# The mixer of a four-layer block makes y by channels, with two heads side by side in TensorE, and VectorE masks the attention maxima

## The chip, the cores and the metric

The kernel runs on one core of a Trainium2 chip. The metric is the device time of one execution in microseconds (us), from its first to its last instruction and the little that lies around them. The kernel before took 2301.28 us (median of 3 runs, 2294.27 to 2305.86).

## The reference

1024 tokens (two sequences of 512) of width 512 go through four layers, each as x = layernorm(x + layer(x)): causal attention with 32 heads of 16, a linear layer with summed binary weights, a state-space mixer, and a linear layer with two chosen low-rank experts. The change touches the attention and, mostly, the mixer. The mixer, per sequence, with H = 128 heads of P = 64 channels, state N = 128, and 8 groups that share B and C (the kernel works in chunks of 128 tokens where the reference has 32; the sum is the same):

```
dt  = softplus(dt + dt_bias);  cum = cumsum(dt * A) inside a chunk
scores[i,j,h] = (C_i . B_j) * exp(cum_i - cum_j) * dt_j      for j <= i
y[i,h,:]      = sum_j scores[i,j,h] * x[j,h,:]               # inside the chunk
              + exp(cum_i,h) * (C_i . state_h)               # carried from earlier chunks
              + D_h * x[i,h,:]
state_h      <- exp(cum_last) * state_h + sum_j dt_j exp(cum_last - cum_j) x_j B_j
g = y * silu(gate);  g = g * rsqrt(mean over the group of g^2 + eps) * norm_w
out = g @ out_w.T
```

x, B and C come out of a projection, a causal convolution with four taps and a SiLU. The gate is another projection of the same input.

## The kernel before

Every engine runs its own program, written out by hand, and they meet only at semaphores. After the attention (16 passes, one for each sequence and key head, to about 306 us) and the linear layer (to about 418 us) comes the mixer, lines 1079 to 1613, to about 2214 us, and then the experts.

The mixer has 8 groups of 16 steps; six of the groups are a loop in the program. A group is two halves of 8 heads (512 channels); a half has 8 chunks of 128 tokens, c = 0 to 7, and c = 0 and c = 4 begin a sequence, so that 12 of 16 steps carry a state in and 12 feed one. I call the steps of a group k = 0 to 15. In a step TensorE does, in this order: for the first half the chunk's B transposed and the product C.B (`cb`, L1269, L1270); the gate of these tokens (`p_gate`, 12 products of fp32r parts, L92); the transposes of the step before's y (`flip_y`, L1240); the carried part C times state for 8 heads at once (`p_inter`, L1284); the projection of one tile of channels for the next half (`p_mix` from `w_x`; in four of 16 steps one of B or C as well); the out-projection of the step before (`p_out`); the new state (`p_state`, L1300); the transposes of the next step's x (`flip_x`, L1231); and the scores times x, one product per head, tokens by 64 channels (`p_intra`, L1310).

Tokens lie on the partitions in y, so the sum with D x (`xskip`) and the product with the gate follow directly (L1539, L1543), and y must be turned into channels (`flip_y`) before it is split into high and low part (`yT`, L1347 and L1441) and projected out. The decays of a step are `cum_all`, 512 KB that a DMA spreads over the partitions, held against the step's own cum by VectorE (`arguments`, L1431), through Exp on ScalarE (8 instructions, L1368), times cb on GpSimd (L1596). ScalarE needs its Exp table for these and its Silu table for the gate and for x (L1375, L741), so it loads a table twice in every step. The first step of each half also splits the half's out-weights (`out_low_part` on VectorE, L1412), the last one the next half's gate weights (`gate_low_part` on GpSimd, L1563).

In the attention (lines 98 to 570) the row maxima are taken from scores that TensorE masks by adding a product of an identity and a mask (L276); VectorE reduces a bank that holds one or two heads (`read_fill`, L445). The scores that become probabilities are made apart, the other way round, and masked likewise (L288). The maxima of the next pass are made while this pass runs: `columns` (L455, L457) ends them, and `flip_max` (L266) needs them.

## Time and profile before

| | |
|---|---|
| median of 3 runs | 2301.28 us |
| the profiled execution | 2301.09 us, its span 2299.3 us |
| TensorE busy | 2129.1 us, 93% |
| VectorE busy | 1659.0 us, 72% |
| ScalarE busy | 1442.3 us, 63% |
| GpSimd busy | 1128.9 us, 49% |
| mean granted TensorE clock | 0.964 |

The profiled execution is one of the same kernel on the chip; its span runs from the first to the last instruction. PE is TensorE (PEld its weight loads), DVE VectorE, ACT ScalarE, POOL GpSimd, SP SyncE, which issues the DMAs. A row of a timeline gives start and length; an x16 merges sixteen instructions, and the time in square brackets is how long the engine had been idle before them and what ended it. A 32-bit product appears as two matmul records, so that the eight heads of L1310 are x16. Two records in a row overlap at their ends, so the cost of work is read from start to next start.

### The profile page before, as it was taken

What the parts mean: (1) busy time and instruction counts of PE and PEld (TensorE: products, weight loads), DVE (VectorE), ACT (ScalarE), POOL (GpSimd) and SP (SyncE); (2) the same over time, 40 slices, a digit from 0 to 9 for tenths busy, and PEclk for the clock granted to TensorE, in tenths of its full rate; (3) what the DMA queues carried; (4) which work ended last, traced back from release to release, by engine and by line L of the source; (5) the groups of instructions that cost most, each with busy time, mean ns of one, the idle gap of its engine ahead of it and who ended that gap; (6) DMA issues with size and microseconds to landing.
All of it is one profiled execution on the core that took longest, in us unless ns stands there. A gap on an engine that the chain in (4) does not pass through costs nothing. (4 is left out here: it accounts for less than half of the span.)

```text
span 2299.3 us, 35192 instructions
## 1 busy us (share of the span) xinstructions
PE 2129.1 (93%) x11224; PEld 1665.0 (72%) x11224; DVE 1659.0 (72%) x2544; ACT 1442.3 (63%) x2823; POOL 1128.9 (49%) x974
## 2 busy tenths in 40 slices
PE   8999997799999999999999999999999999999868
PEld 4666665677778777777787777777777777777645
DVE  4666565678877787778777876787787778777766
ACT  1455523567667766767677667667766776677631
POOL 3444230355555654555555645554656465545531
PEclk9899987899999999999999999999999999999979
DMA  4000010312121212121212122112221222121110
GB/s 156 1 0 0 0 51 19 94 61 92 47 87 56 83 47 88 65 83 41 93 57 83 46 87 83 70 45 89 70 69 62 73 70 72 58 71 59 46 36 37
DMA packets 72235, 140.72 MB, mean 61 GB/s; under 512 B 34449, under 2 KB 35473, under 8 KB 67826
## 3 DMA queue, kind: packets, MB, share of 16 engines
q1 hardware_dynamic: 72050, 138.44, 18.2%
q8 instruction: 93, 1.52, 0.3%
q14 instruction: 92, 0.75, 0.1%
HBM read 134.74 MB, written 3.67 MB: 60 GB/s over the span
## 5 line engine op out<-in xcount | busy, mean ns | idle before, releaser
L92 PE MATMUL p_out<-w_out,yT 128*128 128x512 f32 x1536 | 387.9, 403 | 44.8 <-DVE yT L1441 38.6
L92 PEld LDWEIGHTS p_out<-w_out,yT 128*128 128x128 f32 x1536 | 296.4, 194 | 120.0 <-DVE yT L1441 43.3
L92 PE MATMUL p_mix<-x_high,w_x 128*128 128x512 f32 x1024 | 381.5, 434 | 1.4 <-DVE x_low L1017 1.4
L1596 POOL TENSOR_TENSOR wq_t<-wq_t,cb 128x1024 f32<-128x1024 f32 x128 | 325.0, 2539 | 107.9 <-DVE cb L1486 95.7
L753 DVE SCALAR_TENSOR_TENSOR conv<-p_mix,unit_small,conv 128x511 f32<-128x511 f32 (+2 forms) x384 | 287.2, 748 | 95.0 <-ACT conv L733 85.9
L92 PE MATMUL p_gate<-w_gate,x_high 128*128 128x512 f32 x1024 | 341.4, 415 | 14.8 <-POOL w_gate L1563 14.8
L1368 ACT ACTIVATE wq_t<-wq_t,minus_cum 128x128 f32<-128x128 f32 x1024 | 313.9, 389 | 1.4
L741 ACT ACTIVATE x_channels<-conv 128x512 f32<-128x512 f32 x128 | 80.7, 630 | 266.6 <-DVE conv L753 265.9
L1310 PEld LDWEIGHTS p_intra<-x_dt,wq_t 128*128 128x128 f32 x2048 | 241.2, 192 | 2.4
L1310 PE MATMUL p_intra<-x_dt,wq_t 128*128 128x64 f32 x2048 | 242.7, 272 | 0.0
L1441 DVE TENSOR_TENSOR yT<-p_flip,yT 128x512 fp32r<-128x512 f32 x128 | 88.4, 691 | 213.6 <-ACT yT L1347 213.6
L92 PEld LDWEIGHTS p_mix<-x_high,w_x 128*128 128x128 f32 x1024 | 193.7, 189 | 61.9 <-issue 22.2
L92 PEld LDWEIGHTS p_gate<-w_gate,x_high 128*128 128x128 f32 x1024 | 190.5, 196 | 53.1 <-POOL w_gate L1563 17.0
L1584 POOL TENSOR_TENSOR x_to_state<-x_tokens,group_dt_end 128x512 f32<-128x512 f32 x96 | 102.8, 1071 | 245.3 <-ACT x_tokens L1339 233.9
L1431 DVE TENSOR_TENSOR wq_t<-cum_all,group_logs 128x1024 f32<-128x1024 f32 x128 | 219.4, 1714 | 2.6 <-DMA cum_all<-cum_rows 1.3
L772 POOL TENSOR_TENSOR w_x<-w_raw_tiles,w_x 128x512 fp32r<-128x512 f32 x64 | 87.4, 1366 | 251.1 <-DVE w_x L761 251.0
L92 PE MATMUL p_gate<-w_gate,x_low 128*128 128x512 f32 x512 | 207.4, 405 | 0.0
L92 PE MATMUL p_mix<-x_low,w_x 128*128 128x512 f32 x512 | 201.0, 393 | 0.0
L1588 POOL TENSOR_TENSOR x_dt<-x_tokens,group_dt 128x512 f32<-128x512 f32 x128 | 144.3, 1127 | 99.6 <-PE p_intra L1310 99.3
L1591 POOL TENSOR_TENSOR x_skip<-x_tokens,group_skip 128x512 f32<-128x512 f32 x128 | 182.9, 1429 | 1.0 <-DVE y L1539 1.0
L733 ACT ACTIVATE conv<-p_mix,unit_small 128x512 f32<-128x512 f32 x128 | 99.6, 778 | 114.2 <-PE p_mix L92 112.2
L1375 ACT ACT_TABLE_LOAD x128 | 164.2, 1283 | 5.8 <-DVE y L1543 3.7
(227 smaller groups left out, 4255.0 us busy)
## 6 DMA issues: line engine op xcount, KB each, us to landing
cum_all<-cum_rows SPq DMA_DIRECT2D x128, 512.0 KB, 3.7
w_staged<-in_w_gate SPq DMA_DIRECT2D x16, 1024.0 KB, 5.9
w_raw_tiles<-in_w_x SPq DMA_DIRECT2D x64, 256.0 KB, 3.4
w_staged<-in_w_out SPq DMA_DIRECT2D x16, 1024.0 KB, 4.9
w_raw_tiles<-in_w_bc SPq DMA_DIRECT2D x16, 256.0 KB, 2.8
x<-in_x SPq DMA_DIRECT2D x1, 2048.0 KB, 17.4
out<-z SPq DMA_DIRECT2D x8, 256.0 KB, 2.0
wqkv<-in_wqkv SPq DMA_DIRECT2D x4, 384.0 KB, 6.3
```

The lines of the kernel that those rows point to most:

```text
L92: last = pe.matmul(dst, left[a](k), right[b](k), start=k == 0 and n_ == 0, stop=stop and k == tiles - 1 and n_ == 2)
L733: act.activation(self.conv[:, par], self.p_mix[:, bank], ACT.Identity, bias=w[:, TAPS:TAPS + 1], scale=w[:, TAPS - 1:TAPS]).then_inc(self. ...
L753: m = dve.scalar_tensor_tensor(self.conv[:, par, back:], self.p_mix[:, bank, 0:SEQ - back], w[:, TAPS - 1 - back:TAPS - back], self.conv[: ...
L1310: m = pe.matmul(p_intra[:, h * HEAD_P:(h + 1) * HEAD_P], decay[:, k % 2, h], xdt[:, h], start=True, stop=True)
L1368: m = act.activation(decay[:, k % 2, h], decay[:, k % 2, h], ACT.Exp, bias=neg[:, c, head:head + 1])
L1375: act.activation(sg[:], p_gate[:], ACT.Silu).then_inc(sg_done, 1)
L1431: dve.tensor_tensor(decay[:, k % 2], cumB[:], over(logs[:, 0, c, mine], P), ALU.min).then_inc(arg_done, 1)
L1441: dve.tensor_tensor(yT[:, 1].rearrange("p j t -> p (j t)"), p_flip[:], yT[:, 0].rearrange("p j t -> p (j t)").bitcast(F32), ALU.subtract). ...
L1584: pool.tensor_tensor(xs[:], xtok[:], over(dtend[:, c, mine], HEAD_P), ALU.mult).then_inc(xs_done, 1)
L1588: pool.tensor_tensor(xdt[:], xtok[:], over(dtg[:, c, mine], HEAD_P), ALU.mult).then_inc(xdt_done, 1)
L1591: pool.tensor_tensor(xskip[:], xtok[:], over(dg[:, mine], HEAD_P), ALU.mult).then_inc(xskip_done, 1)
L1596: pool.tensor_tensor(decay[:, k % 2], decay[:, k % 2], cb[:, c].unsqueeze(1).to_broadcast([P, UNIT_HEADS, P]), ALU.mult).then_inc(decay_do ...
```

## The change

In the mixer y is made with channels on the partitions. Each head's product is turned round: x (times dt) is the stationary operand, 64 columns wide, and the head's 128 x 128 scores stream through. Even heads write partitions 0 to 63 of the new bank `p_y`, odd heads 64 to 127. The carried state goes the same way into the same bank, as eight products of state (64 columns) with `Ce`, which is C times exp(cum): exp(cum) is written to DRAM once, at the end of the linear layer, fetched with 512 KB per step, and multiplied by C on GpSimd. So `p_inter`, two VectorE passes over it and the addition are gone, and `flip_y` with them. In exchange the gate is flipped: after SiLU, TensorE transposes it back into its own bank `p_gate`, from where VectorE multiplies it into y; `p_gate` is therefore free only when y is done. The sum of squares, before one ScalarE instruction with an accumulator, is now Square on ScalarE, a reduction over four tiles on VectorE, and a product with a column of ones on TensorE (`sum_squares`). y is one buffer where it was two.

The order of a step changes too. The projection of x channels comes first in it, cb has its own bank, ScalarE does the decays of an even step in the odd step before, after its `last_tap`, and those of an odd step at the end of the even step before, so that a table is loaded once per step; `out_sum` moves behind y. One B/C projection moves from step 0 to step 2.

In the attention the mask products of the maxima go. VectorE adds the mask from a table (`row_mask`) and takes the maximum in one instruction per head, which writes its sum back to PSUM.

```diff
-                        last = pe.matmul(pF[:, b, (i + 1) * wide - P:(i + 1) * wide], ident_b[:], mask_b[:],
-                                         start=False, stop=True)
...
+                        for n_, r in enumerate(heads):
+                            m = dve.tensor_tensor_reduce(pF[:, b, n_ * wide:(n_ + 1) * wide],
+                                                         pF[:, b, n_ * wide:(n_ + 1) * wide],
+                                                         row_mask[:, CPS * P - wide:], 1.0, MASKED, ALU.add, ALU.max,
+                                                         top[:, qc, r:r + 1])
+                        m.then_inc(f_dve, 1)
...
+                sp.wait_ge(soft, 6)
+                for u in range(2 * GROUPS):
+                    sp.dma_start(keep["exp_cum_dram"][u].rearrange("c h t -> h c t"),
...
+                act.activation(dabs[:], cum[:], ACT.Exp, scale=-1.0).then_inc(soft, 1)
...
-                        wait(pe, sg_done, s)
+                        wait(pe, y_done, s)
                         split_product(pe, p_gate[:], ...
...
-                            pe.matmul(p_inter[:], BC[:, 1, cols], state[:].rearrange("p h e -> p (h e)"),
-                                      start=True, stop=True).then_inc(inter_done, 1)
+                            for h in range(UNIT_HEADS):
+                                m = pe.matmul(p_y[sides(h), h // 2], state[:, h], Ce[:, h], start=h < 2, stop=False)
+                            m.then_inc(inter_done, 1)
...
+                        pe.wait_ge(sg_done, s + 1)
+                        for j in range(UT):
+                            m = pe.transpose(p_gate[:, j * P:(j + 1) * P], sg[:, j * P:(j + 1) * P], ident[:])
...
+                            sum_squares(*before)
...
-                            m = pe.matmul(p_intra[:, h * HEAD_P:(h + 1) * HEAD_P], decay[:, k % 2, h], xdt[:, h],
-                                          start=True, stop=True)
+                            m = pe.matmul(p_y[sides(h), h // 2], xdt[:, h], decay[:, k % 2, h],
+                                          start=not carries(c) and h < 2, stop=h >= UNIT_HEADS - 2)
...
+                        if k % 2 and k + 1 < STEPS:
+                            exponentials(s + 1, k + 1)
...
+                        dve.tensor_tensor(y[:], p_y[:], xd[:], ALU.add).then_inc(y_sum, 1)
+                        dve.wait_ge(sg_flipped, s + 1)
+                        dve.tensor_tensor(y[:], y[:], p_gate[:].rearrange("p (j t) -> p j t", j=UT), ALU.mult).then_inc(y_done, 1)
+                        if started and before[1] >= CHUNKS:
+                            out_sum(*before)
...
+                            pool.wait_ge(in_exp_cum, (n_carries(g, k) + 1) * 16)
+                            pool.tensor_tensor(Ce[:], Ce[:], BC[:, 1, cols].unsqueeze(1).to_broadcast([P, UNIT_HEADS, P]),
+                                               ALU.mult).then_inc(ce_done, 1)
```

TensorE, one step of the first half, from one scores product to the next. Before:

```order
L1310 MATMUL p_intra<-x_dt,wq_t 128x64 x8
L1269 MATMUL p_mix<-ident,bc_channels 128x128
L1270 MATMUL p_mix<-bc_channels 128x128
L92 MATMUL p_gate<-w_gate,x_high 128x512 x2
...
L1240 MATMUL p_flip<-ident,y 128x128 x4
L1284 MATMUL p_inter<-state,bc_channels 128x512
L92 MATMUL p_mix<-x_high,w_x 128x512
...
L92 MATMUL p_out<-w_out,yT 128x512 x12
L1300 MATMUL p_state<-x_to_state,b_tokens 128x512
L1231 MATMUL p_flip<-ident,x_channels 128x128 x4
```

And now, in the same step (`wq_t` is the buffer of the decays, `square_sums` the squares summed over four tiles):

```order
L1334 MATMUL p_y<-wq_t,x_dt 64x128 x8
L92 MATMUL p_mix<-x_high,w_x 128x512
...
L1286 MATMUL p_small<-ident,bc_channels 128x128
L1287 MATMUL p_small<-bc_channels 128x128
L92 MATMUL p_gate<-w_gate,x_high 128x512 x2
...
L1301 MATMUL p_y<-c_decayed,state 64x128 x8
L92 MATMUL p_out<-w_out,y_parts 128x512 x12
L1311 MATMUL p_gate<-ident,silu_gate 128x128 x4
L1319 MATMUL p_state<-x_to_state,b_tokens 128x512
L1263 MATMUL p_small<-one_column,square_sums 128x1
L1244 MATMUL p_flip<-ident,x_channels 128x128 x4
```

The x projection went from the middle of the step to its start, the out-projection stands where it stood in time, and behind it now come the gate's transposes, which wait for ScalarE.

ScalarE, an odd step (between two Silu of gates). Before:

```order
L1368 ACT_TABLE_LOAD
L1368 ACTIVATE wq_t<-wq_t,minus_cum 128x128 x8
L1375 ACT_TABLE_LOAD
L1375 ACTIVATE silu_gate<-p_gate 128x512
L1344 REGISTER_ALU
L1347 ACTIVATE yT<-p_flip 128x512
L1349 ACTIVATE y,sum_squares<-y 128x512
```

And now, from the end of an even step through the odd one:

```order
L1371 ACT_TABLE_LOAD
L1371 ACTIVATE wq_t<-wq_t,group_logs 128x128 x8
L1385 ACTIVATE y_parts<-y 128x512
L722 REGISTER_ALU
L724 ACTIVATE conv<-p_mix,unit_small 128x512
L1368 REGISTER_ALU
L1371 ACTIVATE wq_t<-wq_t,group_logs 128x128 x8
L1389 ACTIVATE y<-y 128x512
L1435 ACT_TABLE_LOAD
L1435 ACTIVATE silu_gate<-p_gate 128x512
```

Two steps' decays now stand in a row ahead of the odd step's Silu, and one table load of each kind serves two steps.

VectorE, where a half's first step ends (k = 8) and the next begins:

```order
L1585 TENSOR_TENSOR y<-p_y,x_skip 128x512
L1588 TENSOR_TENSOR y<-y,p_gate 128x512
L1466 SCALAR_TENSOR_TENSOR w_out<-w_staged,unit_small,w_out 128x512 x4
L1485 TENSOR_TENSOR wq_t<-cum_all,group_logs 128x1024
L1494 TENSOR_TENSOR y_parts<-y,y_parts 128x512
```

This order is as before (L1539, L1543, L1412, L1431, L1441); what changed is that the arguments in its fourth row now feed decays that ScalarE makes ahead of its Silu.

## Rows read from the trace of the kernel before

**Rows 1.** The mixer: window, length, busy us of PE, PEld, DVE, ACT, POOL (records), clock, DMA.
```profile
424.00:2214.00 1790.00, 1698.23 (x8544) 1360.86 (x8545) 1356.27 (x1892) 1237.88 (x2414) 963.66 (x679) 0.98 0.21 68
```

**Rows 2.** TensorE's waits in the mixer: us in total, times, longest us.
```profile
PE p_out L92 <- DVE yT L1441: 38.6, 18, 3.5
PE p_flip L1240 <- ACT x_tokens L1339: 18.4, 24, 1.2
PE p_gate L92 <- POOL w_gate L1563: 14.8, 7, 5.0
```

**Rows 3.** Timeline, TensorE, an ordinary step: start us, us, line, shapes, count.
```profile
1216.14 1.02 PE L1300 MATMUL p_state<-x_to_state,b_tokens 128*128 128x512 f32 x2
1216.99 0.60 PE L1231 MATMUL p_flip<-ident,x_channels 128*128 128x128 f32 x4
1217.43 1.90 PE L1310 MATMUL p_intra<-x_dt,wq_t 128*128 128x64 f32 x16
1219.14 0.71 PE L92 MATMUL p_gate<-w_gate,x_high 128*128 128x512 f32 x2
...
1221.99 0.60 PE L1240 MATMUL p_flip<-ident,y 128*128 128x128 f32 x4
1222.42 1.02 PE L1284 MATMUL p_inter<-state,bc_channels 128*128 128x512 f32 x2
```

**Rows 4.** Timeline, TensorE, 32-column products of attention, and what follows.
```profile
149.87 2.36 PE L299 MATMUL pO<-probsT,v_ones 128*32 128x512 f32 x32
152.17 0.63 PE L266 MATMUL pF<-ident,max_cols 128*68 128x128 f32 x4
```

**Rows 5.** Timeline, TensorE, the start of a group of 16 steps.
```profile
1095.55 0.65 PE L1231 MATMUL p_flip<-ident,x_channels 128*128 128x128 f32 x4 [1.52 <-ACT x_channels L741]
...
1098.61 1.22 PE L92 MATMUL p_gate<-w_gate,x_high 128*128 128x512 f32 x2 [2.08 <-POOL w_gate L1563]
...
1103.76 0.60 PE L1240 MATMUL p_flip<-ident,y 128*128 128x128 f32 x4
```

**Rows 6.** Timeline, VectorE, the first step of a half ends, k = 8.
```profile
1221.24 6.45 DVE L1412 SCALAR_TENSOR_TENSOR w_out<-w_staged,unit_small,w_out 128x512 fp32r<-128x512 f32 x4
1227.61 1.21 DVE L1431 TENSOR_TENSOR wq_t<-cum_all,group_logs 128x1024 f32<-128x1024 f32 x1
```

**Rows 7.** Timeline, ScalarE, the same place.
```profile
1222.12 2.46 ACT L1368 ACTIVATE wq_t<-wq_t,minus_cum 128x128 f32<-128x128 f32 x8
1224.59 1.28 ACT L1375 ACT_TABLE_LOAD   x1
1225.89 0.60 ACT L1375 ACTIVATE silu_gate<-p_gate 128x512 f32<-128x512 f32 x1
1226.38 0.59 ACT L1347 ACTIVATE yT<-p_flip 128x512 fp32r<-128x512 f32 x1
```

**Rows 8.** Timeline, VectorE, row maxima of one pass of attention.
```profile
151.09 0.18 DVE L457 SCALAR_TENSOR_TENSOR max_cols<-row_max,max_cols 128x16 fp32r<-128x16 f32 x1
...
156.80 2.15 DVE L445 TENSOR_REDUCE row_max<-pF 128x2 f32<-128x256 f32 x4 [0.57 <-PE pF L276]
...
163.71 1.29 DVE L445 TENSOR_REDUCE row_max<-pF 128x1 f32<-128x512 f32 x2 [0.41 <-PE pF L276]
165.03 0.18 DVE L455 TENSOR_SCALAR max_cols<-row_max 128x16 fp32r<-128x16 f32 x1
```

**Rows 9.** Groups by line and shape: busy us, mean ns, idle before, releaser.
```profile
L1596 POOL TENSOR_TENSOR wq_t<-wq_t,cb 128x1024 f32<-128x1024 f32 x128 | 325.0, 2539 | 107.9 <-DVE cb L1486 95.7 <-ACT wq_t L1368 11.5
...
L1349 ACT ACTIVATION_READ_ACCUMULATOR y<-y 128x1 f32 x128 | 25.9, 202 | 0.0
```

**Rows 10.** Timeline, SyncE's queue, ScalarE and TensorE, before and at the mixer's start.
```profile
394.08 5.66 SPq L859 DMA_DIRECT2D cum_rows<-cum  x16
...
417.17 0.63 ACT L741 ACTIVATE bc_channels<-conv 128x512 f32<-128x512 f32 x1 [1.86 <-DVE conv L753]
...
424.78 1.23 PE L92 MATMUL p_gate<-w_gate,x_high 128*128 128x512 f32 x2 [4.95 <-POOL w_gate L1563]
```


## What I predict, and why

> **What bounds the kernel now.** I read the busy times by stretch first, then TensorE's waits, then the timelines of single steps. The mixer takes 1790 us of 2299.3, and TensorE is busy for 1698 of them [rows 1], so it bounds this stage and waits only some 92 us. The reader should see that 95% of the stage can be changed only by changing TensorE's own work, and that the other engines (1356, 1238 and 964 us) matter where they come late. The list of waits says where that is: 38.6 us for the low part of y, 18.4 for ScalarE to free the transposes' bank, 14.8 for the gate weights of a new half [rows 2]. At the start of a group the timeline has 1.52 and 2.08 us of idle time, and then the gate's 12 products take 5.15 us, from 1098.61 to 1103.76, with the clock fallen to the lower of its two levels [rows 5]. In the ordinary step the gate's products take 2.85 us, 1219.14 to 1221.99 [rows 3]. I call a stage's sum a ledger per group; there are eight groups.
>
> **TensorE's own work in a step.** Prices go from start to next start [rows 3]. The scores times x: 1217.43 to 1219.14, 1.71 us for 16 records, 0.107 each. The carried part has the shape of the state product, two records of 512 columns: 0.85 us (1216.14 to 1216.99). Four transposes: 0.44 us (1216.99 to 1217.43), 0.11 each. The flips of y go and the flips of the gate come, 0.44 against 0.44.
>
> Turned round, a head has 128 columns to stream and not 64, in two records. A 512-column record costs 0.425, so 128 columns cost 0.107, and eight heads one after the other would cost 16 x 0.107 = 1.71 us, the same as now. If two heads run side by side it is 0.85. The trace has such products in the attention: 32 records, four heads in 32 columns each, 512, 384, 256 and 128 columns long, in 2.36 us [rows 4]. One after the other these 1280 columns for four heads in two records would be 8 x 1280/512 x 0.425 = 8.5 us; side by side 2.13. So they run side by side, and I take 0.85 us for two halves of the array. The next product of full width starts 2.30 us after the first narrow one, 0.17 above 2.13. That is the price of leaving the narrow form, some of which (0.11) is the last record's own streaming beyond what I count; entering it is not shown by a row, since attention waits for ScalarE there. The nearest row for a drained engine is that a record of 1.90 us of work for 1.71 us of starts ends 0.19 after the next begins [rows 3]; so entry lies between 0 and 0.19, and I take 0.27 for a visit, with 0.12 and 0.36 as ends.
>
> What the Trainium skill says of this, in TensorEngine Tiling (Array Packing), Key Properties, is that changing the tiling mode drains the engine, not only a change of tile. By that rule the entry is paid in full. Its price here would be the 0.19 above, and the visits' sum 0.36 each; without it 0.12. The rows here show the way out alone, so the rule stands untested for the way in, and it speaks against this change, which makes 224 visits.
>
> So, over 128 steps, of which 96 carry: scores 128 x (1.71 - 0.85 - 0.27) = -75 us. Carried part 96 x (0.85 + 0.27 - 0.85) = +26. Sum of squares: one product with one column, two records that each load 128 columns of weights; the transposes' 0.11 each is the nearest row, 0.22 a step, +28. Together -21 us of TensorE work. With visits at 0.12 it is -55, at 0.36 -1.
>
> **Waits of TensorE in the mixer.** What goes, per group: the flips of y waited 18.4/8 = 2.3 for their bank [rows 2]; x has it alone now. At the group's start 1.52 + 2.08 of idle time and 2.3 of slow clock [rows 5] go as they are, since the x projection now stands ahead of the gate. The waits for y's low part (38.6/8 = 4.8) and some 1.9 of slow clock behind them (my estimate, less than the 2.3 of rows 5) end too, to be counted anew. Sum 14.9.
>
> What comes. I lay a step out from T, the end of a scores product. y is summed and multiplied in 1.6 us of VectorE (1024 columns cost 1.21 [rows 6], the rest is for semaphores), which the x projection covers (12 products like the gate's: 2.75 when nothing is waited for), so the new wait of the gate for `y_done` costs nothing in a plain step. In a half's first step VectorE then splits the out-weights for 6.45 us, and the arguments take 1.21 more [rows 6]; with GpSimd less busy the split is shorter at k = 0, so I put the arguments' end at T + 9.1. y's low part follows at 9.8, against an out-projection that is due at 2.75 + 0.25 for cb (two short products of 0.11 and a little) + 2.85 for the gate + 1.1 for the carried part = 6.9: a wait of 2.9. Behind it ScalarE, which took the decays of the step after next (2.46) only at 9.1, makes y's high part (0.59), loads a table (1.28) and makes the Silu (0.5 from start to next start) [rows 7], by T + 13.9, while the gate's flips are due at 6.9 + 2.9 + 2.75 = 12.6: 1.3 more. So 4.2 us at k = 1 and 4.2 at k = 9. At k = 15 the decays wait for the next group's tables behind `out_sum` and the logs, and Silu is 1.7 late. At k = 8 the gate weights are late by 2.2, since GpSimd now has C times exp(cum), 2.5 us as for the decays [rows 9], and D x ahead of them. At k = 0 I leave 2.7 of the 3.6 us that stood idle there [rows 5], as the loop's own branch and refetch, which no change of order covers, and 0.8 for cb: 3.5. In the other odd steps Silu is ready at T + 9.5 with 9.4 to 9.6 wanted: 0.9 in all. Slow clock after the two long waits: 1.0. Sum 17.7, or 2.8 more than what goes: +22 us. The mixer so comes out at +1.
>
> Not on the path: 96 more products on GpSimd, 96 x 2.54 = 244 us on top of 964 in 1790 [rows 1, 9]; the fetch of C's factor, which by the same layout has some 7 us for 512 KB; ScalarE's 1.28 of table load per step, which it gains as slack.
>
> **The mixer's ends.** Before it, exp(cum) needs a table load of 1.28 and about 1.1 us on ScalarE behind its last Silu, which started at 417.17, and then 16 DMA issues; the 16 of cum took 5.66 us of SyncE's queue [rows 10]. The mixer starts 8 us later. Its first gate waited until 424.78 for weights, 4.95 us idle, and 2.75 us of x projection now fill that. At the end the sum of squares and `out_sum` come one after another, an estimated 1.4. Together +7 (4 to 10).
>
> **The attention.** One pass's maxima on VectorE take from 156.80 to 165.03, 8.2 us, with waits for TensorE among them (0.57 and 0.41 in two rows) [rows 8]. The next pass's first transposes started at 152.17 though the maxima's columns were done at 151.27: TensorE was the later one by 0.9 us [rows 4, 8]. Without the masks TensorE is earlier, so VectorE's chain is late next. Sixteen single maxima: they read 4 x 1280 = 5120 columns. 512 columns cost 0.54 in the row of four (2.15/4) and 0.65 in that of two (1.29/2), so 5.4 to 6.5; I take 6.4, since half of the new ones are shorter than that. Each new instruction has a second one that reads the accumulator out. VectorE has no such row; ScalarE's takes 0.20 [rows 9] and its next starts about 0.1 later. Bounds are 0.05 and 0.35, and I take 0.15: 2.4 us, with 0.4 for counters. That is 9.2, 1.0 longer than now, less the 0.9 of slack, and a little for semaphores: +0.3 a pass, +5 us in 16. With 0.05 it is -15, with 0.35 +50 (3.2 x 16).
>
> For the same instruction the Trainium skill, Vector Engine (DVE) Microarchitecture Reference, section 5.2, gives 1.04 ns per column and about 75 ns per instruction. An estimate by that page is 5.3 + 32 x 0.075 = 7.7 us and the attention would gain about 13 us, the kernel end at 2294.
>
> **Sum.** 2301.1 (the profiled execution; the median of the runs is 2301.3) - 21 + 22 + 7 + 5 = 2314. I say 2312.
>
> **The rivals.** 1. *TensorE gains what it should.* A visit costs 0.12 and not 0.27, -34 us, and the new waits come to no more than the old ones, -22: 2314 - 56 = 2258. For it: 2.30 us against a floor of 2.13 is all that a row shows of the cost of a visit, and ScalarE, relieved of 128 x 1.28 us, is seldom late. Against it: the waits are worked out from places where ScalarE and VectorE are in series.
> 2. *VectorE becomes the bound of attention.* Reading out each maximum costs 0.35, and a pass takes 3 us longer: 2312 + 46 = 2358, slower. It decides from the point where sixteen maxima take over 9.1 us. For it: VectorE is in series with the flips now. Against it: small VectorE instructions in a row are short (L457 0.18).
> 3. *The flipped gate holds TensorE.* Each odd step waits 1 us for Silu behind two steps' decays: 7 more per group, +50: 2362. For it: the margin is 0.1 us. Against it: only if every instruction of ScalarE runs at its lone length.
> 4. *Two heads do not run side by side.* Then each of 224 visits costs 0.85 more, +190: 2502. The 2.36 us speak against it.
>
> **How the numbers follow.** The forecast of 2312 (2290 to 2335 by itself) has 0.36, rival 1 0.32, rival 2 0.16, rival 3 0.13, rival 4 0.03. 0.5% is 11.5 us, about what a measurement can tell from no change; so same is 2290 to 2313. Faster: 0.30 of rival 1, 0.05 of the forecast, 0.01 of others, 0.36. Same: 0.16 of the forecast and 0.04 of the rest, 0.20. Slower 0.44. The range of 2245 to 2368 leaves out the lower tail of rival 1, rival 4 and what of rivals 2 and 3 goes together.
>
> **What would show it.** From a step's first scores record to the next product: 1.1 us (0.95 if rival 1, 2.0 if rival 4). The sum-of-squares product costs 0.22. TensorE's waits in the mixer are near 110 us, most of them for y's low part and the Silu at k = 1 and 9. The mixer begins near 426. An attention pass takes 14.4 us and not 14.1; VectorE stands without a gap in its maxima. I am wrong if TensorE waits for C's factor, if the gate waits for y in plain steps, or if table loads are still two per step.

## The result, and the profile after

The changed kernel takes 2466.39 us (median of 4 runs, 2464.25 to 2470.53) against 2299.41 us before on the same chip: a ratio of 1.0736, 95% interval 1.0706 to 1.0766. I had forecast 2312 us with a range up to 2368. Slower was the likeliest direction by a little, but for a loss of this size I had only the case in which two heads do not run side by side, and that is not what happened.

| stage of the profiled execution | before | after | difference | forecast |
|---|---|---|---|---|
| to the first product behind the attention | 299.3 | 282.0 | -17.3 | +5 |
| from there to the first scores product | 136.5 | 138.2 | +1.7 | +7 with the end |
| mixer, first to last scores product | 1771.3 | 1953.9 | +182.6 | +1 |
| the rest, to the end of the span | 92.2 | 94.7 | +2.5 | |

The mixer on the changed kernel, window, length, busy us of PE, PEld, DVE, ACT, POOL (records), clock, DMA; it answers to [rows 1]:

```profile
413.00:2385.00 1972.00, 1743.69 (x10137) 1345.02 (x10137) 1611.12 (x1821) 1067.75 (x2156) 1240.42 (x774) 0.95 0.27 87
```

In this window, which is 182 us longer than that of [rows 1], VectorE is busy for 1611 us where it was 1356, and GpSimd for 1240 where it was 964. TensorE's busy time grew by only 45, and its mean granted clock fell from 0.98 to 0.95. TensorE's waits, us in total, times, longest us, answer to [rows 2]:

```profile
PE p_out L92 <- DVE y_parts L1494: 92.3, 43, 3.9
PE p_out L92 <- issue: 56.6, 15, 5.4
PE p_gate L92 <- POOL w_gate L1610: 25.6, 11, 2.7
PE p_mix L92 <- POOL w_x L763: 12.2, 16, 0.9
PE p_gate L1311 <- ACT silu_gate L1435: 11.8, 17, 1.3
```

The wait of the out-projection for y's low part is 92.3 us where it was 38.6. The row below it, with "issue", is the same wait at k = 9 and k = 1: the out-projection at 1285.18 starts 0.1 us after VectorE's low part ended at 1285.08, and has no other releaser. So 149 us, where it was 45 before. The flips of y are gone, as foreseen; the gate's flips wait 11.8 us in all. Two rows are waits for GpSimd itself, for weights that it splits: 37.8 us, where it was 14.8.

I add the mixer up over the 127 steps between the first and the last scores product: idle gaps of TensorE 221 us (before 87), everything else 1732 (before 1682). The 50 us of the second part are the granted clock. It stands at the lower of its two levels for 188 us of this stretch, where it did for 68 before, and TensorE is busy for 172 and 61 of them. The twelve records of the out-projection at k = 9 take 5.46 us at the lower level (it fell at 1284.5, while TensorE stood idle, and rose at 1291.3), and 2.91 in another step at the upper one. If I put the cost of the lower level at half of the busy time in it, which is an estimate, it is 86 us where it was 31: 55 more. The rest of the work is then some 5 us less than before.

**TensorE's own work.** The timeline around two scores products (start us, us):

```profile
1338.31 0.28 PE L1263 MATMUL p_small<-one_column,square_sums 128*128 128x1 f32 x2
1338.45 0.63 PE L1244 MATMUL p_flip<-ident,x_channels 128*128 128x128 f32 x4
1339.01 1.09 PE L1334 MATMUL p_y<-wq_t,x_dt 128*64 128x128 f32 x16
1340.04 0.50 PE L92 MATMUL p_mix<-x_high,w_x 128*128 128x512 f32 x1
1340.37 0.39 PE L92 MATMUL p_mix<-x_low,w_x 128*128 128x512 f32 x1
...
1345.46 0.39 PE L92 MATMUL p_gate<-w_gate,x_low 128*128 128x512 f32 x1
1345.78 1.09 PE L1301 MATMUL p_y<-c_decayed,state 128*64 128x128 f32 x16
1346.80 0.50 PE L92 MATMUL p_mix<-x_high,w_bc 128*128 128x512 f32 x1
1347.14 0.39 PE L92 MATMUL p_mix<-x_low,w_bc 128*128 128x512 f32 x1
```

The scores take 1.03 us to the next start (1340.04 - 1339.01), and the first wide record behind them starts its successor after 0.33 where a record in a row needs 0.23: 0.10 more. In front of them 0.20 us pass from the start of the last flip to the first scores record, in every step, where 0.11 passed before: 0.09 more. That is 1.22 in all. The carried product costs 1.02 and loses 0.09 in front of it (1345.46 to 1345.78, where 0.23 is usual) and 0.11 behind it: 1.22 as well. The forecast had 1.12 for each, 0.85 and 0.27 for the visit to narrow products; the 0.37 measured is the upper end that I gave (0.36). The sum of squares is 0.14 us, and the flip behind it takes 0.03 longer than its followers: 0.17, forecast 0.22. With these prices the three terms are 128 x (1.22 - 1.71) + 96 x (1.22 - 0.85) + 128 x 0.17 = -5 us, forecast -21. Two heads do run side by side, but a visit costs more than I took. The Trainium skill says in TensorEngine Tiling (Array Packing), Key Properties, that a change of mode drains the engine. The rows agree: the way in costs 0.09 us in front of both kinds of narrow product, and the way out 0.10 to 0.11.

**Where the time went.** A step of a second half, k = 10, VectorE:

```profile
1294.89 0.69 DVE L1588 TENSOR_TENSOR y<-y,p_gate 128x512 f32<-128x512 f32 x1
1295.50 0.75 DVE L1516 SCALAR_TENSOR_TENSOR acc<-p_out,inv_rms,acc 128x512 f32<-128x512 f32 x1
1296.28 2.55 DVE L1519 SCALAR_TENSOR_TENSOR acc<-attn,inv_rms,acc 128x512 f32<-128x512 f32 x1
1298.75 3.40 DVE L1485 TENSOR_TENSOR wq_t<-cum_all,group_logs 128x1024 f32<-128x1024 f32 x1
1302.07 1.52 DVE L1494 TENSOR_TENSOR y_parts<-y,y_parts 128x512 fp32r<-128x512 f32 x1
1303.52 0.74 DVE L744 SCALAR_TENSOR_TENSOR conv<-p_mix,unit_small,conv 128x511 f32<-128x511 f32 x1
```

and GpSimd in the same time:

```profile
1294.88 1.04 POOL L1636 TENSOR_TENSOR x_dt<-x_tokens,group_dt 128x512 f32<-128x512 f32 x1
1295.88 2.40 POOL L1640 TENSOR_TENSOR c_decayed<-c_decayed,bc_channels 128x1024 f32<-128x1024 f32 x1
1298.24 2.83 POOL L1645 TENSOR_TENSOR wq_t<-wq_t,cb 128x1024 f32<-128x1024 f32 x1
1301.03 2.02 POOL L1649 TENSOR_TENSOR x_skip<-x_channels,group_skip 128x512 f32<-128x512 f32 x1
```

The reader should lay the two over each other. The second pass of `out_sum` (L1519) starts at 1296.28, while C's product runs from 1295.88 to 1298.28. It ends at 1298.83, 0.55 us behind the end of C's product, and takes 2.55 us where it takes 0.75 alone (its lone length: what it takes when GpSimd is idle). The arguments (L1485) start at 1298.75, while the decays run from 1298.24 to 1301.07, and end at 1302.15, 1.08 us behind them: 3.40 for work of 1.21. y's low part (L1494) starts at 1302.07, while D x runs to 1303.05, and ends 0.54 us behind it: 1.52 for 0.68. Two passes ahead of them, y times gate (L1588, 0.69) and the sum from `p_out` (L1516, 0.75), keep their length, though GpSimd works beside them as well. GpSimd is held too: D x takes 2.02 us where its shortest is 1.03, and ends 0.90 us behind the arguments. TensorE waits for the end of this row of passes:

```profile
1285.18 5.46 PE L92 MATMUL p_out<-w_out,y_parts 128*128 128x512 f32 x12 [4.79 <-issue]
...
1303.65 0.73 PE L92 MATMUL p_out<-w_out,y_parts 128*128 128x512 f32 x2 [2.91 <-DVE y_parts L1494]
```

Groups over the whole kernel show the same (mean ns is the number behind the busy us):

```profile
L1485 DVE TENSOR_TENSOR wq_t<-cum_all,group_logs 128x1024 f32<-128x1024 f32 x128 | 278.0, 2172 | 2.5 <-DVE group_logs L1475 1.2 <-DMA cum_all<-cum_rows 1.2
L1494 DVE TENSOR_TENSOR y_parts<-y,y_parts 128x512 fp32r<-128x512 f32 x128 | 170.5, 1332 | 8.5 <-ACT y_parts L1385 8.5
L1519 DVE SCALAR_TENSOR_TENSOR acc<-attn,inv_rms,acc 128x512 f32<-128x512 f32 x64 | 127.5, 1993 | 2.3
L744 DVE SCALAR_TENSOR_TENSOR conv<-p_mix,unit_small,conv 128x511 f32<-128x511 f32 x128 | 94.7, 740 | 13.9 <-ACT conv L724 13.9
L1588 DVE TENSOR_TENSOR y<-y,p_gate 128x512 f32<-128x512 f32 x128 | 88.2, 689 | 13.7 <-DVE y L1585 0.5
```

Taps and the product with the gate read one operand from PSUM and stay at 740 and 689 ns. The arguments, y's low part and the second pass of `out_sum` read two operands from SBUF. Of the 128 low parts, the 48 that had no GpSimd product beside them took 676 to 686 ns, the other 80 took 1522 to 2889 ns (counted from start and end of every record of both engines). All 80 end 0.55 us behind the GpSimd product that ran when they started; so do the 55 second passes of `out_sum` that are lengthened, and 77 of the arguments end 1.08 us behind it. Casts of x weights, with one SBUF operand, took 411 to 422 ns in 32 cases and 1837 to 1867 in the other 32, which end 0.28 us behind a GpSimd product; the reduction of the squares, with one SBUF operand too, is hardly lengthened (1036 to 1086 ns alone, 1037 to 1104 beside GpSimd). The Trainium skill, SBUF — State Buffer, section "SBUF: two separate sides", says that VectorE and GpSimd share one pair of ports, held by one of them for a whole instruction, and that a VectorE instruction takes part in it when it has two SBUF inputs or runs in a two-port mode. The rows agree: a long pass ends its lone length, or a little less, behind the GpSimd product that was running.

The kernel before shows it as well, in rows that I did not read for the prediction:

```profile
L1431 DVE TENSOR_TENSOR wq_t<-cum_all,group_logs 128x1024 f32<-128x1024 f32 x128 | 219.4, 1714 | 2.6 <-DMA cum_all<-cum_rows 1.3 <-DVE group_logs L1422 1.2
L1441 DVE TENSOR_TENSOR yT<-p_flip,yT 128x512 fp32r<-128x512 f32 x128 | 88.4, 691 | 213.6 <-ACT yT L1347 213.6
L1462 DVE SCALAR_TENSOR_TENSOR acc<-attn,inv_rms,acc 128x512 f32<-128x512 f32 x64 | 48.1, 752 | 2.2
L1505 DVE TENSOR_TENSOR x_skip<-x_skip,y 128x512 f32<-128x512 f32 x96 | 83.9, 874 | 3.3
```

The arguments had a mean of 1714 ns and not the 1.21 us that [rows 6] show, and the low part, from PSUM, 691. The change moved y's low part from the class of passes that do not care to the class that does, and put 257 us more of GpSimd work beside it. It did two more things to this class. The second pass of `out_sum` (L1462) always had two SBUF operands, but it stood where GpSimd was idle and took 752 ns every time; in its new place behind y it takes 1993. And y times gate went the other way, from 982 ns with the gate in SBUF (L1543) to 689. The time that VectorE's passes in the mixer take beyond the shortest of their kind is 180 us before and 404 now: 224 of the 255 us by which VectorE is busier.

**The attention.** The maxima of a pass (VectorE; the ACCUMULATOR row reads out the maximum):

```profile
149.16 0.30 DVE L448 CUSTOM_DVE_ANT_0 pF<-pF,row_mask 128x128 f32<-128x128 f32 x1 [0.70 <-PE pF L276]
149.38 0.14 DVE L448 DVE_READ_ACCUMULATOR2_ANT row_max<- 128x1 f32 x1
149.38 0.33 DVE L448 CUSTOM_DVE_ANT_0 pF<-pF,row_mask 128x128 f32<-128x128 f32 x1
...
155.66 0.73 DVE L448 CUSTOM_DVE_ANT_0 pF<-pF,row_mask 128x512 f32<-128x512 f32 x1
156.31 0.14 DVE L448 DVE_READ_ACCUMULATOR2_ANT row_max<- 128x1 f32 x1
...
156.70 0.18 DVE L464 SCALAR_TENSOR_TENSOR max_cols<-row_max,max_cols 128x16 fp32r<-128x16 f32 x1
```

They take 7.5 us from 149.16 to 156.70, not the 9.2 of the forecast: the reading out takes 0.14 us, but the next maximum starts at the same moment. Each costs 0.65 us for 512 columns and 0.25 for 128, which is 1.04 ns a column and 0.12 us besides, read-out included. The passes come every 12.9 to 13.0 us instead of 14.15. `flip_max` (L268) starts 0.55 us after VectorE has ended the columns (143.67 + 0.18), where it was 0.9 before: VectorE is nearer to holding it, and TensorE is still the later one. The 32-column products cost 2.30 us as in [rows 4]:

```profile
142.11 2.36 PE L299 MATMUL pO<-probsT,v_ones 128*32 128x512 f32 x32 [0.20 <-ACT probsT L410]
144.40 0.63 PE L268 MATMUL pF<-ident,max_cols 128*68 128x128 f32 x4
```

The estimate by the Trainium skill, Vector Engine (DVE) Microarchitecture Reference, section 5.2, was 7.7 us a pass. The page gives its prices for VectorE's operations in general, and not for this instruction by name. The rows agree with the price of a column, and nearly with the fixed one: 0.12 us for a maximum and its read-out, where the estimate took twice 0.075.

### The profile page after: what moved, and what is told of

Same layout as the page of the kernel before. It is cut to its first block and busy times, and to the rows that moved or that the text cites. A ratio compares the mean times of both kernels' runs of the same rounds, so it can differ in the third digit from the quotient of the medians.

```text
span 2468.8 us, 38015 instructions
## 1 busy us (share of the span) xinstructions
PE 2153.0 (87%) x12568; PEld 1629.3 (66%) x12568; DVE 1923.9 (78%) x2793; ACT 1275.1 (52%) x2570; POOL 1407.9 (57%) x1072
## 5 line engine op out<-in xcount | busy, mean ns | idle before, releaser
L92 PE MATMUL p_out<-w_out,y_parts 128*128 128x512 f32 x1536 | 446.7, 447 | 148.9 <-DVE y_parts L1494 92.3
L92 PEld LDWEIGHTS p_out<-w_out,y_parts 128*128 128x128 f32 x1536 | 324.2, 216 | 243.3 <-DVE y_parts L1494 104.2
L1371 ACT ACTIVATE wq_t<-wq_t,group_logs 128x128 f32<-128x128 f32 x1024 | 313.9, 389 | 157.8 <-DVE wq_t L1485 156.5
L1485 DVE TENSOR_TENSOR wq_t<-cum_all,group_logs 128x1024 f32<-128x1024 f32 x128 | 278.0, 2172 | 2.5 <-DVE group_logs L1475 1.2
L1640 POOL TENSOR_TENSOR c_decayed<-c_decayed,bc_channels 128x1024 f32<-128x1024 f32 x96 | 257.1, 2678 | 0.0
L1649 POOL TENSOR_TENSOR x_skip<-x_channels,group_skip 128x512 f32<-128x512 f32 x128 | 179.4, 1402 | 0.0
L1494 DVE TENSOR_TENSOR y_parts<-y,y_parts 128x512 fp32r<-128x512 f32 x128 | 170.5, 1332 | 8.5 <-ACT y_parts L1385 8.5
L1389 ACT ACTIVATE y<-y 128x512 f32<-128x512 f32 x128 | 79.7, 623 | 167.9 <-DVE y_parts L1494 167.9
L1585 DVE TENSOR_TENSOR y<-p_y,x_skip 128x512 f32<-128x512 f32 x128 | 88.1, 688 | 84.9 <-PE p_y L1334 84.9
L1500 DVE TENSOR_REDUCE square_sums<-y 128x128 f32<-128x512 f32 x128 | 136.8, 1069 | 9.6 <-ACT y L1389 9.6
L1364 ACT ACTIVATE x_tokens<-p_flip 128x512 f32<-128x512 f32 x128 | 75.5, 590 | 130.5 <-PE p_flip L1244 130.5
```

The costliest lines, as they stand in the source:

```text
L92: last = pe.matmul(dst, left[a](k), right[b](k), start=k == 0 and n_ == 0, stop=stop and k == tiles - 1 and n_ == 2)
L1371: m = act.activation(decay[:, k % 2, h], decay[:, k % 2, h], ACT.Exp, scale=-1.0, bias=minus_cum[:, c, head:head + 1])
L1485: dve.tensor_tensor(decay[:, k % 2], cumB[:], over(minus_cum[:, c, mine], P), ALU.max).then_inc(arg_done, 1)
L1494: dve.tensor_tensor(yT[:, 1], y[:], yT[:, 0].bitcast(F32), ALU.subtract).then_inc(y_low, 1)
L1500: dve.tensor_reduce(sq[:], y[:].rearrange("p j t -> p t j"), AX_X, ALU.add).then_inc(sq_done, 1)
L1585: dve.tensor_tensor(y[:], p_y[:], xd[:], ALU.add).then_inc(y_sum, 1)
```

## The experiments

Two theories for the mixer, by their short names. **Port** (for the ports that the two engines share): GpSimd's added products lengthen VectorE's passes over two SBUF operands, and y's low part is one of them now. **Order**: VectorE has more passes in series between y and its low part, `out_sum` above all. Rivals: TensorE's visits to 64 columns, GpSimd itself late, ScalarE late with the flipped gate. All runs are compared with the kernel before on the same chip.

| run | median us | ratio, 95% interval |
|---|---|---|
| the changed kernel | 2466.4 | 1.0736 (1.0706 to 1.0766) |
| 1 attention of after, mixer of before | 2282.3 | 0.9929 (0.9903 to 0.9955) |
| 2 second pass of out_sum late | 2389.5 | 1.0403 (1.0355 to 1.0452) |
| 3 without C's product | 2312.1 | 1.0058 (1.0034 to 1.0081) |
| 4 before, more GpSimd | 2399.4 | 1.0437 (1.0387 to 1.0488) |
| 5 as 2, low part first | 2445.5 | 1.0629 (1.0586 to 1.0673) |
| 6 C's product late | 2694.4 | 1.1709 (1.1659 to 1.1758) |
| 7 all order changes | 2723.1 | 1.1833 (1.1775 to 1.1892) |
| 8 as 7, without C's product | 2562.5 | 1.1145 (1.1097 to 1.1192) |
| 9 D x on ScalarE | 2435.7 | 1.0581 (1.0523 to 1.0639) |
| 10 as 9, second pass late | 2375.7 | 1.0327 (1.0271 to 1.0382) |
| 11 as 3, second pass late | 2292.7 | 0.9963 (0.9933 to 0.9993) |

**1. The attention alone.** In the kernel before, the attention (lines 98 to 570 of the new one) is taken from the changed kernel:

```diff
-                        dve.tensor_reduce(top[:, qc, heads[0]:heads[-1] + 1], src, AX_X, ALU.max).then_inc(f_dve, 1)
+                        for n_, r in enumerate(heads):
+                            m = dve.tensor_tensor_reduce(pF[:, b, n_ * wide:(n_ + 1) * wide],
...
```

> The mixer of before with the attention of after. Both theories of the mixer leave this run alone; it separates attention from mixer. The attention passes should keep the 12.9 to 13.0 us of the changed kernel (14.15 before), so the first product behind the attention starts 17 us earlier, and the mixer keeps its 1771 us from first to last scores: 2299 - 17 = 2282 us (2278 to 2287). If the shorter attention only paid because of something in the new mixer's tables, it would be 2299.

2282.29 us, as expected. It is the version that beats both kernels, the one before by 0.7%.

**2. The second pass of out_sum behind the taps.**

```diff
                         if started:
                             add_squares(*before)
+                        if not (first and k < 2) and earlier[1] >= CHUNKS:
+                            out_sum_second(*earlier)
```

> The changed kernel with the second pass of out_sum (kept half times rms) taken from between y's product and the arguments and put behind the next step's taps. Order theory: this pass stands in series ahead of y's low part in the 8 steps of each second half, 64 times, at 1.8 to 2.55 us: 64 x 2.1 = -134, of which a fifth comes back at Silu: 2466 - 110 = 2356 us, waits of p_out for y's low part down from 149 (with those shown as issue) to some 50 us. Port theory alone (the pass is long only because GpSimd works beside it, and what follows it takes over the crowded time): only its lone 0.75 us goes, 64 x 0.75 = -48: 2418 us, and the arguments stay at a mean of 2.17 us or rise. Rival that TensorE's own 64-column visits are the loss: no change, 2466.

2389.45 us, 77 less than the changed kernel, between the two expectations (2356 and 2418). Waits of the out-projection:

```profile
PE p_out L92 <- DVE y_parts L1494: 54.8, 29, 3.6
PE p_out L92 <- issue: 52.9, 15, 5.4
```

They fell from 149 to 108 us, not to 50. The pass itself got short (1043 ns from 1993), but y's low part took its place beside GpSimd's products: 1791 ns, where it was 1332. Moving a pass away moves the next one into the crowded time, so the port holds back some of what the order gives. The time of VectorE's passes beyond the shortest of their kind hardly fell, from 404 to 394 us; what helps is where it falls.

**3. Without C's product on GpSimd.**

```diff
-                            pool.tensor_tensor(Ce[:], Ce[:], BC[:, 1, cols].unsqueeze(1).to_broadcast([P, UNIT_HEADS, P]),
-                                               ALU.mult).then_inc(ce_done, 1)
+                            pool.tensor_tensor(Ce[:, 0, 0:2], Ce[:, 0, 0:2], BC[:, 1, c * P:c * P + 2],
+                                               ALU.mult).then_inc(ce_done, 1)
```

> The changed kernel without C's product on GpSimd (2 columns of 1024 multiplied, so the carried part is computed from exp(cum) alone; DMA, semaphores and all other work stay). Port theory: VectorE's passes over two SBUF operands get shorter, the arguments from a mean of 2.17 to some 1.7 us and y's low part from 1.33 to under 1.0, and with them the waits of p_out: -60 to -110, 2380 us. Order theory: VectorE's order is unchanged, so 2466 within 8 us, and the means stay. If GpSimd's own lateness were the cause (decays late), TensorE's waits for decays would have to shrink, but they are 1 us in the trace, so nothing.

2312.12 us: 154 of the 167 us come back, more than I expected (the product with C is left out, so the carried part is not the right one). VectorE's program is the same, but its passes are shorter (arguments, low part), and so are TensorE's waits:

```profile
L1485 DVE TENSOR_TENSOR wq_t<-cum_all,group_logs 128x1024 f32<-128x1024 f32 x128 | 210.3, 1643 | 2.4 <-DVE group_logs L1475 1.2 <-DMA cum_all<-cum_rows 1.1
L1494 DVE TENSOR_TENSOR y_parts<-y,y_parts 128x512 fp32r<-128x512 f32 x128 | 141.8, 1108 | 34.3 <-ACT y_parts L1385 34.3
```

```profile
PE p_out L92 <- DVE y_parts L1494: 37.4, 28, 3.6
PE p_out L92 <- issue: 28.6, 15, 3.3
```

1643 and 1108 ns where it was 2172 and 1332; 66 us of waits where it was 149. Order theory, which wanted 2466 here, falls as the only cause. TensorE's idle gaps in the mixer are 123 us, and all else is 1671 us, 61 less than in the changed kernel with the same products in the same order. That is the clock: its lower level costs 30 us here by the estimate above, where it cost 86, and its mean in the mixer is 0.98 again.

The rival that GpSimd is late by itself can be read off the waits. VectorE waits for nothing of GpSimd's in the mixer of the changed kernel. TensorE's waits for weights that GpSimd splits fell from 37.8 to 20.3 us: 17 of the 98 us of idle gaps that went. The waits for y's low part gave 83.

**4. More GpSimd work in the kernel before.**

```diff
+                        if carries(c):
+                            for i in range(2):
+                                pool.tensor_tensor(xdt[:], xtok[:], over(dtg[:, c, mine], HEAD_P), ALU.mult).then_inc(again, 1)
```

> The kernel before with x times dt made three times instead of once on GpSimd in the 96 carrying steps (same values; 2.2 to 2.5 us of GpSimd work more, 211 to 240 us, near the 257 us of C's product). Port theory: the arguments (two SBUF operands) rise from a mean of 1.71 to 2.1 us or more while y's low part (a PSUM operand, 0.69) does not move; the kernel slows by 10 to 40 us. Rival that more GpSimd work is simply hidden: 2299 within 5 us and the arguments stay at 1.71.

2399.4 us, 104 slower than before: far over my 10 to 40. The passes over two SBUF operands:

```profile
L1432 DVE TENSOR_TENSOR wq_t<-cum_all,group_logs 128x1024 f32<-128x1024 f32 x128 | 232.6, 1817 | 2.3 <-DVE group_logs L1423 1.2 <-DMA cum_all<-cum_rows 1.0
L1506 DVE TENSOR_TENSOR x_skip<-x_skip,y 128x512 f32<-128x512 f32 x96 | 171.6, 1788 | 18.0 <-POOL x_skip L1597 15.1
L1442 DVE TENSOR_TENSOR yT<-p_flip,yT 128x512 fp32r<-128x512 f32 x128 | 88.3, 690 | 231.4 <-ACT yT L1348 231.4
```

The sum with D x went from 874 to 1788 ns and the arguments from 1714 to 1817, less than I expected; y's low part, with its PSUM operand, stayed at 690. So the old mixer, with no other change, loses six tenths of what the new one lost when GpSimd gets as much more to do (the added products took 263 us). Not all of it is the port: 15 us of the waits of VectorE are for D x itself, which GpSimd then finishes late, and TensorE waits 5 us more for gate weights. Against these 20 us stand 108 by which the time of VectorE's passes beyond their shortest grew (180 to 288). How much of either reaches the end, this run does not part.

**5. y's low part ahead of the arguments** (with 2):

```diff
+                        if started:
+                            y_low_part(*before)
                         if k + 1 < STEPS:
                             arguments(s + 1, k + 1)
...
-                        if started:
-                            y_low_part(*before)
                         conv("x")
```

> The changed kernel with the second pass of out_sum behind the taps (as in the run before) and y's low part ahead of the next step's arguments on VectorE. Order theory: the arguments (2.07 us on average) leave the path to the out-projection in every step that waits for it (k = 1, 9, 10, 11, 14, 15 and a little elsewhere), some 1.5 to 2 us in each of five steps of a group, and give back up to 1.5 at the Silu of odd steps, where the arguments now end later: 2389 - 8 x 5 = 2349 us. Port theory alone: nearly the same VectorE work is crowded into the same time of GpSimd, y's low part itself now stands beside C's product and gets longer (1.79 to 2.2 us), so 2389 - 15 = 2374 us.

2445.49 us, 56 slower than run 2, against both expectations. The waits moved:

```profile
PE p_gate L1311 <- ACT silu_gate L1435: 116.8, 56, 4.9
PE p_out L92 <- issue: 25.6, 7, 3.7
```

The arguments, now later, feed decays that stand ahead of the Silu on ScalarE in odd steps, and the gate's flips wait 116.8 us where it was 11.8. This is the third rival of the prediction, with the condition that it needs: it was not the cause in the changed kernel, but it is next in line. What the earlier low part gives is taken back there.

**6. C's product as GpSimd's last one, the carried product next to the scores.**

```diff
+                        if carries(c):
+                            pe.wait_ge(state_done, n_feeds(g, k))
+                            pe.wait_ge(ce_done, n_carries(g, k) + 1)
...
                         pe.wait_ge(decay_done, s + 1)
```

> The changed kernel with C's product as the last of GpSimd's products in a step, behind the decays and D x, the carried product directly ahead of the scores on TensorE (so that a step has one visit to 64 columns and not two), and the new state taken by VectorE behind y's low part. The same GpSimd work in all. Port theory: GpSimd's C product now runs beside the taps, which read PSUM and keep 747 ns, and not beside out_sum, arguments and y's low part: these shorten (arguments from 2.17 to 1.8, second pass of out_sum from 1.99 to 1.5), about -90, and TensorE saves 96 entries and exits of 0.2 to 0.3 us, -24: 2350 us. If only GpSimd's sum of work counts (VectorE is slowed by as much wherever the product stands): -24 and a little, 2440 us. If the carried product now comes late, TensorE waits for GpSimd at p_y and the time is over 2466.

2694.39 us. The port part was right: the arguments fell to 1659 ns, the second pass of `out_sum` to 1297. But the third case of the expectation came true, and a fourth thing with it:

```profile
PE p_y L1327 <- issue: 159.4, 48, 4.1
DVE wq_t L1484 <- DMA cum_all<-cum_rows: 137.2, 55, 4.6
```

All 48 of the carried product's waits end 0.10 us behind the end of C's product on GpSimd (at 1542.93 the carried product starts, C's product ran from 1540.50 to 1542.83), which now stands behind the decays and D x. So the carried product is late by GpSimd's chain, and the scores behind it too.

The other row is a queue. `c_decayed` is one buffer. Its next fetch waits on SyncE's queue for the carried product (`inter_done`), which now ends a step and not its middle; the fetch of the next step's `cum_all` stands behind it in the queue:

```profile
1502.26 0.33 SPq L698 DMA_DIRECT2D cum_all<-cum_rows  x1
...
1544.28 0.33 SPq L1229 DMA_DIRECT2D c_decayed<-exp_cum_rows  x1
1544.86 0.55 SPq L698 DMA_DIRECT2D cum_all<-cum_rows  x1
```

In a step without the fetch the row of `cum_all` starts by itself; in this one it comes 0.58 us behind the fetch of `c_decayed`, when the scores are already running (from 1543.98), and VectorE waits 137 us in all for it. In 54 of the 55 waits a fetch of `c_decayed` stands directly ahead.

**7 and 8. All order changes, and the same without C's product.** The edits of 2, 5 and 6 together; in 8 also that of 3.

> All of the order changes together: second pass of out_sum behind the taps, y's low part ahead of the arguments, C's product last on GpSimd, carried product next to the scores, new state late. If the causes are the ones named (VectorE's series behind y, and the port), the idle time of TensorE in the mixer falls from 221 to near the 90 of before, and own work stays: 2300 us (2280 to 2330). If a third cause holds part of the loss, it stays over 2350.

> The run with all order changes, and C's product on GpSimd left out (2 columns of 1024, so the carried part comes from exp(cum) alone). What is left is the change without its GpSimd price and in the better order. Port theory: another 30 to 60 us below the run with the product, 2255 us; if order had taken all of the crowding away, within 10 us of it.

2723.05 and 2562.46 us, both far over what I expected. They inherit the late chain of 6 and the Silu of 5 (168.6 and 174.7 us of waits for it), so neither says anything on a good order of the new mixer. The difference of 161 us between them is near the 154 of run 3, but it is no second measurement of the same price: in this order the carried product waits for C's product directly, 131 us in run 7 and 39 in run 8, and the lower clock level, by the estimate above, costs 192 and 126 us.

**9 and 10. D x on ScalarE.** Nothing is left out of the computation:

```diff
-                        pool.tensor_tensor(xd[:], X[:, :, cols], over(dg[:, half * UT:(half + 1) * UT], P),
...
+                        for j in range(UT):
+                            m = act.activation(xd[:, j], X[:, j, c * P:(c + 1) * P], ACT.Copy, scale=dg[:, at_:at_ + 1])
```

> The changed kernel with D x made by ScalarE (four instructions of 128 columns with a scale by channel, behind the step's conversions of B and C) and not by GpSimd; nothing is left out. GpSimd loses 179 us of work, ScalarE gains some 130. Port theory: C's product cost 154 us for 257 us of GpSimd work beside VectorE; D x stands later, mostly beside y's low part and the taps, so it should give back a third of its 179 us, 60 us: 2406 us, with y's low part from 1.33 down to near 1.0 us and the reader seeing no D x beside it. If the loss of the run without C's product came from GpSimd's own lateness, taking D x away (nobody waits for it) brings nothing, and ScalarE's added work makes it slower: 2470 us or more.

> The same, and the second pass of out_sum behind the taps. Port and order together: the first gave -77 by itself, D x some -60, partly the same waits: 2389 - 40 = 2350 us. If the two act on the same waits wholly, 2389 or 2406, whichever is less.

2435.68 us, 31 less than the changed kernel (expected 60), and 2375.68, 14 less than run 2 (expected 40). Nobody waits for D x in the changed kernel, and yet taking it off GpSimd makes the kernel faster though ScalarE gets more to do. It does so in two ways: the second pass of `out_sum` falls from 1993 to 1735 ns, and the waits for y's low part from 149 to 120 us, which is the port; and TensorE's waits for x weights from GpSimd fall from 12.2 to 1.7, which is GpSimd's own lateness. The size was too high: y's low part went only from 1332 to 1311 ns, since the decays still run beside VectorE's passes.

**11. Without C's product, second pass late.** The edits of 3 and 2.

> The second pass of out_sum behind the taps, and C's product on GpSimd left out (2 columns of 1024). The run with the product left out alone took 2312, the run with the pass moved alone 2389. In the first the second pass of out_sum still took 1.59 us in 64 steps, 102 us; half of it should come back: 2312 - 45 = 2267 us. If the port was all, nothing is left to gain: 2312. TensorE's own work in the mixer should stay at 1618 to 1630 us in every run.

2292.65 us, 20 less than run 3 (expected 45). The mixer takes 1775 us from first to last scores product, 108 of them idle gaps. All else is 1668 us where the kernel before has 1682, and 5 of these 14 us are the clock. So with the port relieved and the order mended, TensorE's own work is some 9 us less than before, between the 5 by the measured prices and the 21 forecast, and the idle gaps eat it: the new mixer is then no faster than the old one, and the kernel is 10 us behind run 1. (The 1618 to 1630 us that I expected for TensorE's own work in every run are not met: all else less the cost of the clock lies between 1617 and 1661 us.)

## Why the prediction was wrong

- *TensorE's own work, -21 us.* The mechanism was right, the price of a visit too low: 1.22 with its products, forecast 1.12, 224 times. The sum of squares cost 0.17 (0.22). Worked out from the rows -5, in run 11 -9.
- *"Not on the path: 96 more products on GpSimd, 244 us on top of 964 in 1790."* This is the step that failed. The work was priced by GpSimd's room alone (it took 257 us), and not by what runs beside it on VectorE. Leaving it out gives back 154 us; adding 263 us of such work to the kernel before costs 104. A small part is GpSimd's own lateness: TensorE's waits for it grew from 14.8 to 37.8 us.
- *The waits, +22 us.* Measured: idle gaps +134 us, and all else +50, of which the work itself is -5: some 55 us are the lower clock level behind the gaps, for which I had 1.0 us a group to come and 4.2 to go. I laid the step out with the arguments at 1.21 and the low part at 0.7, both lone lengths. The places that I laid out were near, in part by luck: at k = 9 I had 2.9 + 1.3 us and the waits are 4.9 and none; at k = 8 2.2 and 2.7. What I had at nothing or next to it, k = 10, 11, 13 and 14, has 2.9, 2.4, 1.3 and 1.9 us in the mean, and k = 15 3.6 instead of 1.7. These are the steps in which `out_sum`, arguments and low part come one after another beside GpSimd. [Rows 6] show 1.21 for the arguments, in the one step in which a long split stands ahead of them; the group row had 1714 ns.
- *out_sum ahead of the low part.* I had it only at the mixer's end and at k = 15. It stands in 64 steps, and moving half of it away gives 77 us. That half took 752 ns in its old place and takes 1993 in the new one.
- *The attention, +5 us.* Wrong sign, -17: a pass's maxima with their read-outs take 7.5 us and not 9.2, 0.12 us each over the 1.04 ns a column, where I had added 0.15 for the read-out to a dearer column. Run 1 confirms the gain by itself. My other sums there were loose: 7.7 us a pass gives -19 us by my own working and not the -13 that I wrote.
- *The rivals.* TensorE gains: its work did gain a little, its waits did not. VectorE the bound of the attention: no. The flipped gate: 11.8 us, not 56 or more, but it appears when the arguments come later (run 5). Two heads not side by side: no, though its 2502 is the nearest number.

What stays open: how the 104 us of run 4 divide between the port and GpSimd's own lateness; how the changed kernel's loss divides between port and order, since the same pass belongs to both; and whether a second buffer for C's factor would make the late product pay, which wasn't tried.

## What to carry to other kernels

Price work that is moved to GpSimd by what VectorE does in that time: here a VectorE pass over two SBUF operands waited for the end of the GpSimd product beside it, and one with an operand in PSUM did not. A pass that moves in the order can land beside such a product too. When a result moves from PSUM to SBUF, the passes that read it change class, though their lone length stays. And take durations from the group's mean and its two ends, not from one row: a mean of 1714 ns beside a row of 1.21 us is the sign that something else holds the engine.

## What was not expected of the hardware

- VectorE's passes over two SBUF operands have steps, not a smooth growth: y's low part takes 0.68, 1.52 or up to 2.89 us, the arguments 1.21 to 3.41 us. A cast with one SBUF operand went from 0.42 to 1.85 us, a reduction of an operand of the same size stayed at 1.04 to 1.10. GpSimd's D x went from 1.03 to 2.02 us by the same meeting.
- The read-out of an accumulator on VectorE (0.14 us) starts at the same moment as the next maximum; the two instructions together cost 0.12 us over the price of the columns.
- A fetch that waits for a late consumer on SyncE's queue delays the next fetch behind it, which has nothing to do with that consumer: 137 us of waits for `cum_all` in run 6.
